# A graph-network kernel on one NeuronCore: new hand-written step orders for three engines

## The chip, the cores and the metric

The kernel runs on one core of a Trainium2 chip. A core has five engines that run their own instruction streams side by side: TensorE (PE in the profile), VectorE (DVE), ScalarE (ACT), GpSimd (POOL) and SyncE (SP, which here only issues loads). They tell each other by semaphores that a buffer is ready or free. The metric is device time in microseconds (us) of one execution; less is better. All 64 graphs are computed by this one core.

## The reference, cut to what matters

The input is 64 graphs of 128 nodes with 64 features each, a 0/1 adjacency matrix per graph, and a node mask. Four graph layers follow one another, each with a residual and a normalisation over the features:

```
x = layernorm(x + PNA(x, adj))            # mean, max, min, std over the neighbours; then a linear layer
x = layernorm(x + adj @ (x @ W) + bias)
x = layernorm(x + MLP(x + quantiles(x, dilated adj)) * mask)   # 0.25/0.5/0.75 quantiles over few neighbours
x = layernorm(x + (adj + I) @ x / rowsum)
```

Max and min over the neighbours (layer 1) and the quantiles over the neighbours (layer 3) are the costly parts: both gather each node's neighbours by rank with one-hot matmuls. Layer 3 then sorts up to 11 gathered values with a sorting network.

## The kernel before

The 64 graphs are worked on in eight groups of eight; the code calls a group a turn, t0 to t7. Every layer of a turn is cut into steps, small functions that each issue some instructions on one engine. Three strings at the top of the file, `TENSOR_ORDER`, `SCALAR_ORDER` and `VECTOR_ORDER`, write out the order of the steps on the three engines; `GPSIMD_ORDER` and `SYNC_ORDER` do so for the other two. An entry `name:which@lag` means: in round number n, do step `name` of turn n+lag. So `so:0-20@-1` is the first twenty operations of the sort of the turn before the round's number. Each round repeats the string, entries that name no turn from 0 to 7 are left out, and rounds begin and end so that every step of each turn is done once. This is a software pipeline: while layer 1 of one turn is begun, layers 1 and 2 of the turn before and layers 3 and 4 of the turn before that are finished.

Nothing but these strings sets the order on an engine. Each step begins with waits on semaphores for what it reads and for buffers to be free; an engine that waits does nothing else, and what stands behind the waiting step waits with it.

The steps that matter here, with the lines that the profile shows for them:

- VectorE. `cm` (L1289) masks the adjacency of the next turn; `gt` (L1295), `P` (L1306 to L1309) build the permutation that sorts nodes by degree; `nb`, `mp` (L1323), `rw` (L1332) prepare masks and row factors. `h0` (13 operations, L1362) and `h2` (11 operations, L1370) write one-hot matrices. `dr` (L1344, L1348) finds the dropped neighbours of the dilation. `ng`, `me`, `we` (L1390 to L1394) close mean and variance. `tr:0`, `tr:1` (L1404, L1418) take max and min over gathered slots. `zf:0`, `zf:1` (L1435, L1436) form layer 1's output. `so` (66 operations, L1479) is the sorting network, `wg:0` to `wg:5` (L1492) weigh ranks, `ag` (L1502, L1506) adds them. `z1`, `z2` (L1536), `z3` add the residuals; `n0d` to `n3d` (L1440) and `n0x` to `n3x` (L1444, L1445) are the two VectorE halves of the four normalisations. `r1`, `r2` split x2 for bf16. `em` (L1355) marks empty slots. `pre:k` are set-up steps that only turn 0 has: among them `pre:2` (tables), `pre:3` (weights of the ranks, L1263 to L1282), `pre:4` (degrees of the other 48 graphs, L1143, L1144).
- ScalarE. It empties PSUM and takes squares and roots: `e0:0` to `e0:7` (L912) and `e2:0` to `e2:3` (L921) move gathered slots of layers 1 and 3 to SBUF, two halves each; `ys:0`, `ys:1` (L863) scale layer 1's output; `n0q` to `n3q` (L926) square, `n0r` to `n3r` (L930) take the root; `vt` (L796) and `k2` (L801), `sd` (L896, L898), `y2e` (the rows zB<-rest of L839), `z3e`, `xr`, `ac` (L887), `xh`, `xm`, `xl` (parts of x2), `dtc` (L791), `kn` (whose L780 writes dcol), `pm`, `pl`, `up`, `rp`, `qo`.
- TensorE. `g0:0` to `g0:7` and `g2:0` to `g2:3` gather (two halves each, into two PSUM banks that are used in turn, called the ring; a half may start once the half before last has been emptied); `wr:k` put rank weights into the same ring; `yl:0`, `yl:1` layer 1's linear layer (L445 pna<-bdx,xT is its first matmul); `dt`, `va`, `p2` the dilation; `ss`, `mt` mean and variance; `b1`, `b2` layer 2; `c2`, `c3` (L442 rest<-weights,hT) layer 3's MLP; `c6` layer 4; `kc`, `lv` degrees.
- GpSimd, whose order string is not changed. In each round it does `sk@0` (L1085 to L1093, nine small operations: it needs `kn`'s dcol, and VectorE's `dr` needs it) and then `sc@-2` (L1099, eight indirect DMAs that scatter the finished rows xo to DRAM; it needs `n3x` of that turn). So `sk` of turn n stands behind `sc` of turn n-3.

The last turn's `n3x` is followed by its eight scatters and the end of the program.

Of the kernel before, what the change touches and what calls it, by code (L numbers as in the profile page):

```python
# [134 lines left out]
class Turn:  # L135
# [13 lines left out]


TENSOR_ORDER = """
    g0:1@-1 cr@-1 g0:2@-1 g0:3@-1 kc@0 g0:4@-1 lv@0 g0:5@-1 g0:6@-1 g0:7@-1 yl:0@-1 wr:0@-2 wr:1@-2 yr@0 yl:1@-1
    ap@0 b3@-2 pre:0@0 wr:2@-2 wr:3@-2 xt@0 sm@0 qp@0 wr:4@-2 wr:5@-2 b1@-1 p1@0 b2@-1 q1@0 c2:0@-2 c2:1@-2 q2@0
    dt@0 ss@0 c3@-2 g2:0@-1 va@0 g2:1@-1 p2@0 g2:2@-1 g2:3@-1 c6@-2 g0:0@0 mt@0"""
SCALAR_ORDER = """
    adj@0 n0q@-1 xs@0 n0r@-1 kn@0 b3e@-2 qo@0 up@0 b1e@-1 rp@0 n1q@-1 c2e:0@-2 pm@0 n1r@-1 k1@0 xh@-1 pl@0
    c2e:1@-2 xm@-1 dtc@0 xl@-1 ac@0 e2:0@-1 y2e@-2 vt@0 e2:1@-1 sd@0 n2q@-2 e2:2@-1 n2r@-2 k2@0 e2:3@-1 xr@-2
    e0:0@0 z3e@-2 e0:1@0 n3q@-2 pre:0@2 e0:2@0 n3r@-2 sg@0 e0:3@0 e0:4@0 e0:5@0 e0:6@0 mts@0 e0:7@0 pre:1@0
    ys:0@0 pb@1 ysb@1 ys:1@0"""
VECTOR_ORDER = """  # L160
    so:28-32@-2 gt@0 tr:0@-1 so:32-40@-2 P@0 tr:1@-1 so:40-44@-2 zf:0@-1 so:44-66@-2 wg:0@-2 wg:1@-2 pre:0@0
    zf:1@-1 wg:2@-2 nb@0 n0d@-1 wg:3@-2 pre:1@0 mp@0 n0x@-1 rw@0 wg:4@-2 wg:5@-2 ag@-2 z1@-1 dr@0 n1d@-1
    h2:0-1@-1 pre:2@0 n1x@-1 pre:3@0 h2:1-3@-1 r1@-1 h0:0-1@0 h2:3-4@-1 r2@-1 h0:1-2@0 h2:4-6@-1 h0:2-3@0
    h2:6-8@-1 h0:3-4@0 h2:8-11@-1 h0:4-9@0 me@0 ng@0 we@0 z2@-2 n2d@-2 h0:9-13@0 n2x@-2 pre:5@-1 em@0 pre:4@0
    cm@1 so:0-20@-1 z3@-2 so:20-24@-1 n3d@-2 so:24-28@-1 n3x@-2
    pre:6@-2"""
GPSIMD_ORDER = """
    pre:2@0 pre:0@2 sk@0 pre:1@1 sc@-2 pre:3@-1"""
SYNC_ORDER = """
# [1583 lines left out]
```

## Time and profile before

| | |
|---|---|
| median of 3 runs | 649.8 us (649.49 to 651.43) |
| profiled execution, its own time | 646.34 us |
| its span, first to last instruction | 644.8 us |
| mean granted TensorE clock | 0.874 of full |
| busy: PE, PE weight loads | 482.3 us (75%), 320.0 us (50%) |
| busy: DVE | 514.6 us (80%) |
| busy: ACT | 370.4 us (57%) |
| busy: POOL | 112.8 us (17%) |

Busy time is the time in which an engine had an instruction in work. VectorE is the busiest over the span. From the page's 40 slices one sees a start of some 60 us in which set-up runs, six alike stretches, and a tail of some 70 us in which all engines are half idle. The chain that ended last goes 34% over DVE and 22% over PE. In the timelines, the idle time in front of an instruction and what released it stand in brackets; on DVE and ACT an instruction begins some 0.1 us before the one ahead of it ends.

### The profile page before, as it was taken

The numbers are of one execution on the slowest core, as the hardware profiler recorded it, in microseconds if no ns is written. First come the engines' busy times: TensorE is split into PE (matmuls) and PEld (weight loads), VectorE is DVE, ScalarE is ACT, GpSimd is POOL, SyncE is SP. The second block draws the span as 40 slices with busy tenths as digits, with TensorE's granted clock in tenths as the row PEclk, the third lists the DMA queues.
The fourth block names the chain that finished last, engine by engine and source line by source line (L and its number), as shares of the span: only waits on it lengthen the run. The fifth ranks groups of instructions, "written<-read, shape, count | busy, mean of one in ns | idle before, by whom it ended". The sixth has DMA issues, their size and how long they took to land.

```text
span 644.8 us, 10421 instructions
## 1 busy us (share of the span) xinstructions
PE 482.3 (75%) x3380; PEld 320.0 (50%) x3419; DVE 514.6 (80%) x1504; ACT 370.4 (57%) x990; POOL 112.8 (17%) x186
## 2 busy tenths in 40 slices
PE   2467968797988889798979897989888977861420
PEld 2443655365545655475557554755575545440220
DVE  4895639999799978999899989997999799379220
ACT  0264677447874678568855885588558842440230
POOL 4300010301014100510061006100610070006022
PEclk9866998999899989989998999899989997555555
DMA  8400020002000200020002000200000000000000
GB/s 312 162 0 1 2 82 1 2 1 82 2 4 16 81 2 2 17 83 2 2 16 83 2 1 18 83 2 1 17 2 2 2 17 2 1 0 17 0 6 15
DMA packets 6718, 18.32 MB, mean 28 GB/s; under 512 B 1792, under 2 KB 1920, under 8 KB 6144
## 3 DMA queue, kind: packets, MB, share of 16 engines
q1 hardware_dynamic: 4608, 15.48, 6.8%
q0 software_dynamic: 2048, 2.10, 1.1%
q8 instruction: 28, 0.46, 0.3%
q14 instruction: 34, 0.28, 0.1%
HBM read 15.48 MB, written 2.10 MB: 27 GB/s over the span
## 4 chain that ended last, share of the span: by engine, by line
DVE 34%; issue 27%; PE 22%; ACT 8%; POOL 6%; POOLq 0%; DVEq 0%; ACTq 0%
DVE hot L1479 7%; DVE slot L1479 7%; PE pna L445 6%; DVE slot L1404 5%; PE pna L442 5%; POOL out_dram L1099 5%; PE ring L442 4%; PE relab L442 2%; PE rest L442 2%; DVE deg L1143 1%; ACT wv L863 1%; PE ring L655 1%; DVE slot L1502 1%; DVE P L1309 1%; DVE hot L1492 1%
## 5 line engine op out<-in xcount | busy, mean ns | idle before, releaser
L442 PE MATMUL ring<-hot,parts 128*64 128x384 bf16 (+3 forms) x753 | 137.1, 358 | 0.9
L1099 POOL DMA_INDIRECT out_dram<-xo,idx x64 | 78.1, 1220 | 309.9 <-DVE xo L1445 292.9
L912 ACT ACTIVATE slot<-ring 128x512 f32<-128x512 f32 (+1 forms) x128 | 61.6, 525 | 42.6 <-PE ring L442 38.4
L442 PEld LDWEIGHTS ring<-hot,parts 128*128 128x128 bf16 (+1 forms) x768 | 55.5, 107 | 39.6 <-issue 4.1
L863 ACT ACTIVATE wv<-pna,rowP 128x64 f32<-128x64 f32 x128 | 28.0, 329 | 77.6 <-PE pna L442 77.6
L1404 DVE TENSOR_TENSOR slot<-slot 128x128 f32<-128x128 f32 (+2 forms) x144 | 53.1, 424 | 2.8 <-ACT slot L912 0.9
L1479 DVE TENSOR_TENSOR hot<-slot 128x64 f32<-128x64 f32 (+5 forms) x136 | 50.8, 407 | 3.5 <-ACT slot L921 3.5
L445 PE MATMUL ring<-emp,rowsel 112*128 112x512 bf16 (+1 forms) x128 | 45.3, 354 | 10.9 <-ACT slot L912 7.0
L1479 DVE TENSOR_TENSOR slot<-slot 128x64 f32<-128x64 f32 (+5 forms) x136 | 51.2, 406 | 0.0
L445 PE MATMUL pna<-bdx,xT 128*128 128x384 f32 x64 | 28.6, 530 | 16.5 <-DVE zF L1436 16.5
L921 ACT ACTIVATE slot<-ring 128x384 f32<-128x384 f32 x64 | 31.3, 502 | 15.3 <-PE ring L442 15.2
L442 PE MATMUL pna<-weights,QQ 128*128 128x192 f32 x128 | 36.6, 371 | 0.0
L445 PE MATMUL rest<-x2T,weights 128*128 128x512 f32 x32 | 22.3, 785 | 18.1 <-DVE x2T L1506 10.4
L442 PE MATMUL pna<-wmm,slot 128*128 128x192 f32 x128 | 34.5, 354 | 0.0
L1479 DVE TENSOR_TENSOR hot<-hot 128x128 f32<-128x128 f32 (+3 forms) x96 | 33.6, 378 | 0.0
L1085 POOL TENSOR_SCALAR skp<-dcol 128x2 f32<-128x2 f32 x8 | 2.1, 264 | 175.7 <-ACT dcol L780 175.7
L839 ACT ACTIVATE zB<-rest,rowP 128x64 f32<-128x64 f32 x128 | 28.0, 340 | 6.9 <-PE rest L442 4.0
L445 PE MATMUL ring<-sgnT,delta 32*128 32x512 bf16 (+2 forms) x48 | 14.6, 364 | 22.4 <-DVE slot L1492 20.3
L1479 DVE TENSOR_TENSOR slot<-hot 128x64 f32<-128x64 f32 (+5 forms) x88 | 31.3, 378 | 0.0
L1440 DVE TENSOR_REDUCE stB<-sqB 128x8 f32<-128x512 f32 x16 | 10.9, 683 | 25.2 <-ACT sqB L926 25.2
L445 PEld LDWEIGHTS ring<-emp,rowsel 112*128 112x128 bf16 x128 | 12.9, 101 | 33.8 <-ACT slot L912 22.2
L839 ACT ACTIVATE m<-pna,rowP 128x64 f32<-128x64 f32 x128 | 28.7, 394 | 0.1
(280 smaller groups left out, 1139.1 us busy)
## 6 DMA issues: line engine op xcount, KB each, us to landing
Cc<-adj_cols_dram SPq DMA_DIRECT2D x8, 512.0 KB, 3.8
R<-adj_rows_dram SPq DMA_DIRECT2D x8, 512.0 KB, 5.4
slot<-adj_rows_dram SPq DMA_DIRECT2D x4, 1024.0 KB, 12.4
xn<-x_nat_dram SPq DMA_DIRECT2D x8, 256.0 KB, 5.5
out_dram<-xo,idx POOLq DMA_INDIRECT x64
weights<-wpack_dram SPq DMA_DIRECT2D x1, 608.5 KB, 8.0
biasr<-wrows_dram SPq DMA_DIRECT2D x1, 128.0 KB, 9.4
own_loop<-adj_diag_dram SPq DMA_DIRECT2D x1, 32.0 KB, 15.1
```

Of the source, the lines that this page charges most:

```text
L442: return mm(*a, start=False, stop=True, skip_group_check=True, **k)
L445: return mm(*a, start=True, stop=True, skip_group_check=True, **k)
L655: mm(ps[:, OFF2[k] - lo:OFF2[k] - lo + CAP2[k]], fill2[:, k, :, :].rearrange("p a d -> p (a d)"), sgnT[t.n % KEEP][:, c, 0:CAP2[k]], start ...
L839: last = A(dst[:, g, :], src(g), ACT.Copy, scale=rowP[t.n % ROWKEEP][:, g, which:which + 1])
L863: last = A(ys[:, g, f, :], PQ[:, 256 * g + D * (f + 1):256 * g + D * (f + 2)], ACT.Copy, scale=rowP[t.n % ROWKEEP][:, 4 * h + g, AMP + f:A ...
L912: A(slot0[:, g, lo:hi], PG[ring["g0", t.n, 2 * g + j][0]][:, 0:hi - lo], ACT.Copy).then_inc(s["slot0"], 1)
L921: A(slot2[:, c, lo:hi], PG[ring["g2", t.n, 2 * c + j][0]][:, 0:hi - lo], ACT.Copy).then_inc(s["slot2"], 1)
L1099: nc.gpsimd.indirect_dma_start(out=out, out_offset=bass.IndirectOffsetOnAxis(ap=idx[t.n % ROWKEEP][:, g:g + 1], axis=0), in_=xo[:, g, :], ...
L1143: own(V.tensor_reduce(deg[:, k * CHUNK:(k + 1) * CHUNK], chunk[k], AX.X, ALU.add))
L1404: return V.tensor_tensor(dst, dst, src, ALU.max)
L1440: V.tensor_reduce(st[:, 0, :], sq[:, :, :], AX.X, ALU.add).then_inc(s[signal], 1)
L1479: mark(("sort", k), V.tensor_tensor(low if is_min else wire(b, 1 - sb_, width), low, high, ALU.min if is_min else ALU.max))
```

## The change

Three order strings are replaced. No step is added or left out and no step's body is changed; POOL's and SP's strings stay. The whole diff:

```diff
--- before.py
+++ after.py
@@ -149,21 +149,21 @@
 
 
 TENSOR_ORDER = """
-    g0:1@-1 cr@-1 g0:2@-1 g0:3@-1 kc@0 g0:4@-1 lv@0 g0:5@-1 g0:6@-1 g0:7@-1 yl:0@-1 wr:0@-2 wr:1@-2 yr@0 yl:1@-1
-    ap@0 b3@-2 pre:0@0 wr:2@-2 wr:3@-2 xt@0 sm@0 qp@0 wr:4@-2 wr:5@-2 b1@-1 p1@0 b2@-1 q1@0 c2:0@-2 c2:1@-2 q2@0
-    dt@0 ss@0 c3@-2 g2:0@-1 va@0 g2:1@-1 p2@0 g2:2@-1 g2:3@-1 c6@-2 g0:0@0 mt@0"""
+    p2@-1 g0:0@-1 c6@-3 mt@-1 g0:1@-1 cr@-1 g0:2@-1 g0:3@-1 kc@0 g0:4@-1 g0:5@-1 g0:6@-1 lv@0 g0:7@-1
+    yl:0@-1 yr@0 wr:0@-2 pre:0@0 b3@-2 yl:1@-1 wr:1@-2 ap@0 wr:2@-2 xt@0 wr:3@-2 wr:4@-2 sm@0 wr:5@-2 qp@0
+    b1@-1 q1@0 b2@-1 c2:0@-2 q2@0 p1@0 c2:1@-2 ss@0 dt@0 c3@-2 va@0 g2:0@-1 g2:1@-1 g2:2@-1 g2:3@-1"""
 SCALAR_ORDER = """
-    adj@0 n0q@-1 xs@0 n0r@-1 kn@0 b3e@-2 qo@0 up@0 b1e@-1 rp@0 n1q@-1 c2e:0@-2 pm@0 n1r@-1 k1@0 xh@-1 pl@0
-    c2e:1@-2 xm@-1 dtc@0 xl@-1 ac@0 e2:0@-1 y2e@-2 vt@0 e2:1@-1 sd@0 n2q@-2 e2:2@-1 n2r@-2 k2@0 e2:3@-1 xr@-2
-    e0:0@0 z3e@-2 e0:1@0 n3q@-2 pre:0@2 e0:2@0 n3r@-2 sg@0 e0:3@0 e0:4@0 e0:5@0 e0:6@0 mts@0 e0:7@0 pre:1@0
-    ys:0@0 pb@1 ysb@1 ys:1@0"""
+    e0:2@-1 n3q@-3 e0:3@-1 e0:4@-1 e0:5@-1 e0:6@-1 mts@-1 e0:7@-1 pre:1@-1 ys:0@-1 ysb@0 pb@0 b3e@-2 n3r@-3
+    ys:1@-1 adj@0 n0q@-1 xs@0 kn@0 n0r@-1 qo@0 rp@0 b1e@-1 pm@0 up@0 n1q@-1 c2e:0@-2 pl@0 n1r@-1 k1@0 xh@-1
+    c2e:1@-2 dtc@0 xm@-1 ac@0 pre:0@3 xl@-1 y2e@-2 e2:0@-1 n2q@-2 e2:1@-1 n2r@-2 e2:2@-1 vt@0 e2:3@-1 sd@0
+    k2@0 xr@-2 e0:0@0 z3e@-2 e0:1@0 sg@0"""
 VECTOR_ORDER = """
-    so:28-32@-2 gt@0 tr:0@-1 so:32-40@-2 P@0 tr:1@-1 so:40-44@-2 zf:0@-1 so:44-66@-2 wg:0@-2 wg:1@-2 pre:0@0
-    zf:1@-1 wg:2@-2 nb@0 n0d@-1 wg:3@-2 pre:1@0 mp@0 n0x@-1 rw@0 wg:4@-2 wg:5@-2 ag@-2 z1@-1 dr@0 n1d@-1
-    h2:0-1@-1 pre:2@0 n1x@-1 pre:3@0 h2:1-3@-1 r1@-1 h0:0-1@0 h2:3-4@-1 r2@-1 h0:1-2@0 h2:4-6@-1 h0:2-3@0
-    h2:6-8@-1 h0:3-4@0 h2:8-11@-1 h0:4-9@0 me@0 ng@0 we@0 z2@-2 n2d@-2 h0:9-13@0 n2x@-2 pre:5@-1 em@0 pre:4@0
-    cm@1 so:0-20@-1 z3@-2 so:20-24@-1 n3d@-2 so:24-28@-1 n3x@-2
-    pre:6@-2"""
+    so:24-28@-2 z3@-3 so:28-32@-2 pre:3@-1 so:32-35@-2 gt@0 so:35-38@-2 n3d@-3 so:38-40@-2 tr:0@-1
+    so:43-44@-2 so:40-43@-2 P@0 so:44-47@-2 tr:1@-1 zf:0@-1 so:47-66@-2 n3x@-3 wg:0@-2 pre:0@0 zf:1@-1 nb@0
+    wg:1@-2 wg:2@-2 wg:3@-2 wg:4@-2 n0d@-1 pre:1@0 rw@0 wg:5@-2 n0x@-1 ag@-2 mp@0 pre:2@0 z1@-1 h2:0-2@-1
+    n1d@-1 h2:2-3@-1 n1x@-1 dr@0 r1@-1 h2:3-4@-1 ng@0 h2:4-6@-1 h0:0-3@0 r2@-1 h0:3-6@0 h2:6-8@-1 h0:6-7@0
+    h2:8-11@-1 em@0 h0:7-9@0 z2@-2 h0:9-12@0 me@0 n2d@-2 pre:5@-1 h0:12-13@0 we@0 pre:4@0 n2x@-2 cm@1
+    so:0-24@-1 pre:6@-2"""
 GPSIMD_ORDER = """
     pre:2@0 pre:0@2 sk@0 pre:1@1 sc@-2 pre:3@-1"""
 SYNC_ORDER = """
```

The new strings are also cut at another place: the steps from `so:24-28` on, which stood at the end of a round, now stand at the head of the next round with their lag lowered by one. That alone changes nothing in the sequence that an engine sees. What differs in the sequence, with the lags brought to the same round:

- VectorE: `n3x` goes from behind sort operation 28 to behind the whole sort; `tr:0` and `P` stand later against the sort and `zf:0` directly behind `tr:1`; `wg` 1 to 5 stand behind `zf:1` and `nb`; `n0x`, `mp` and `dr` stand later, with `dr` behind `n1x`; `ng`, `em` and most of `h0` stand earlier; between `z2` and `n2d` now stand three `h0` operations and `me`, and `we` stands behind `n2d`. `pre:3` stands in the second round instead of the first.
- ScalarE: `y2e` goes ahead of `e2:0`; `n2q` goes from behind `e2:1` and `sd` to directly behind `e2:0`; `vt` from ahead of `e2:1` to behind `e2:2`, `sd` behind `e2:3`; `xl` behind `ac`; `pm` ahead of `up`; `b3e` and `n3r` between `pb` and `ys:1`.
- TensorE: `va` goes ahead of `g2:0`, `p2` behind `g2:3`; `ss` goes ahead of `dt`; `p1` behind `q2`; `lv` behind `g0:6`; the `wr` steps are spread between `yr` and `qp`, and `b3` goes ahead of `yl:1`.

## Rows read from the trace of the kernel before

**Rows 1.** Engines' busy time in one steady turn: PE, PEld, DVE, ACT, POOL, clock, DMA, GB/s
```profile
441.00:506.00 65.00, 56.01 (x425) 37.64 (x429) 59.14 (x172) 45.18 (x125) 11.92 (x17) 0.97 0.02 6
```

**Rows 2.** Timeline of DVE in that turn: start, duration, line, operation, idle time before
```profile
473.96 0.69 DVE L1492 TENSOR_TENSOR slot<-slot,ring 128x512 f32<-128x512 f32 x1
...
475.74 0.42 DVE L1435 TENSOR_TENSOR zF<-pna,wv 128x256 f32<-128x256 f32 x1 [0.50 <-ACT wv L863]
...
486.97 0.61 DVE L1348 SCALAR_TENSOR_TENSOR drop<-keyN,skp,drop 128x128 bf16<-128x128 bf16 x2
...
488.86 0.69 DVE L1445 TENSOR_TENSOR x<-zF,stF 128x512 f32<-128x512 f32 x1
...
499.29 0.68 DVE L1536 TENSOR_TENSOR zB<-zB,x 128x512 f32<-128x512 f32 x1
503.58 0.69 DVE L1440 TENSOR_REDUCE stB<-sqB 128x8 f32<-128x512 f32 x1 [3.61 <-ACT sqB L926]
...
506.52 0.23 DVE L1479 TENSOR_TENSOR hot<-slot 128x64 f32<-128x64 f32 x1 [0.36 <-ACT slot L921]
```

**Rows 3.** Timeline of ACT around the longest wait of DVE
```profile
497.09 1.75 ACT L839 ACTIVATE zB<-rest,rowP 128x64 f32<-128x64 f32 x8
499.35 1.02 ACT L796 ACTIVATE validT<-relab 128x1024 bf16<-128x1024 f32 x1 [0.52 <-PE relab L442]
...
502.31 0.72 ACT L898 ACTIVATE m<-wv,eps 128x512 f32<-128x512 f32 x1
502.93 0.61 ACT L926 ACTIVATE sqB<-zB 128x512 f32<-128x512 f32 x1
...
505.50 0.98 ACT L921 ACTIVATE slot<-ring 128x384 f32<-128x384 f32 x2
```

**Rows 4.** Timeline of PE: c3, g2:3 and its last half; then a g2 half of the tail
```profile
492.85 1.90 PE L442 MATMUL rest<-weights,hT 128*128 128x64 f32 x16
...
503.98 0.34 PE L655 MATMUL ring<-sgnT,fill 32*128 32x128 bf16 x3 [0.37 <-ACT slot L921]
...
505.19 0.73 PE L442 MATMUL ring<-hot,parts 128*64 128x424 bf16 x6
...
568.12 1.27 PE L442 MATMUL ring<-hot,parts 128*64 128x424 bf16 x6
```

**Rows 5.** Timeline of POOL: first and last scatter of eight, sk, two scatters of later turns
```profile
452.20 1.07 POOL L1099 DMA_INDIRECT out_dram<-xo,idx  x1 [35.05 <-DVE xo L1445]
...
462.63 1.44 POOL L1099 DMA_INDIRECT out_dram<-xo,idx  x1 [0.30 <-issue]
479.20 0.23 POOL L1085 TENSOR_SCALAR skp<-dcol 128x2 f32<-128x2 f32 x1 [15.13 <-ACT dcol L780]
...
481.83 0.20 POOL L1093 TENSOR_TENSOR skp<-skp 128x2 f32<-128x2 f32 x1
...
524.30 3.69 POOL L1099 DMA_INDIRECT out_dram<-xo,idx  x1 [0.30 <-issue]
...
632.97 0.96 POOL L1099 DMA_INDIRECT out_dram<-xo,idx  x1 [0.30 <-issue]
```

**Rows 6.** Busy time and granted clock during yl:1 of turn 2 and of turn 6
```profile
207.30:211.70 4.40, 4.38 (x24) 3.69 (x25) 4.40 (x18) 0.00 (x0) 0.00 (x0) 1.00 0.01 4
467.90:474.00 6.10, 6.10 (x25) 5.21 (x26) 6.07 (x22) 0.04 (x1) 0.00 (x0) 0.72 0.01 4
```

**Rows 7.** Timelines of DVE and ACT in the start
```profile
38.98 0.29 DVE L1263 TENSOR_SCALAR zB<-steps_of 32x2 f32<-32x2 f32 x3
...
41.62 1.11 DVE L1282 TENSOR_SCALAR delta<-zB,parity 32x576 bf16<-32x576 f32 x2
...
57.19 0.93 ACT L912 ACTIVATE slot<-ring 128x512 f32<-128x512 f32 x2 [4.15 <-DVE rtmp L1144]
...
65.04 0.28 DVE L1295 TENSOR_TENSOR gt<-relab,thr 128x112 bf16<-128x112 f32 x1 [7.29 <-PE relab L445]
...
114.33 0.91 DVE L1479 TENSOR_TENSOR hot<-slot 128x64 f32<-128x64 f32 x1 [1.13 <-ACT slot L921]
```

## The prediction, made before the changed kernel was run

> **What bounds the kernel now.** I read the slices of the page first, then the busy time by windows, then the timelines of the engines over one turn. From turn 2 to turn 6 the program repeats itself: the scatter that starts at 452.20 in [rows 5] has its twin one turn earlier at 387.32, and the first sort operations of turns 5 and 6 lie at 441.65 and 506.52, so one turn takes 64.9 us. In 65.0 us DVE is busy for 59.1, PE for 56.0, ACT for 45.2 [rows 1]. So DVE sets the pace, and what it loses is 5.8 us of waits per turn. The timeline shows where [rows 2]: 3.61 us stand in one place, ahead of n2d (503.58), behind ACT's square n2q; 0.50 ahead of zf:1; 0.36 ahead of the sort; two more of 0.41 (wg:4) and 0.22 (r2); the rest is small change between dependent operations, about 0.5, which any order keeps. The square itself is not slow: ACT had y2e done at 498.84 and z2 followed at 499.29 to 499.97, but n2q began only at 502.93, because in ACT's order vt, e2:1 and sd stand between [rows 3], and e2:1 waits for a gather that PE runs behind va. The wait is one of order, not of work. A new order can therefore give back at most about 5.3 us in each steady turn; with no wait left a turn would take 59.2 + 0.5 = 59.7 us.
>
> **The steady turn in the new order.** I lay DVE's steps back to back and ask at each wait whether the other engines have delivered.
>
> *n2q.* y2e is now ahead of e2:0, n2q directly behind it. From the end of y2e, n2q is done after e2:0 (0.98 in [rows 3]) and its own 0.61, some 1.5 us. DVE has z2 (0.68), three small h0 operations (0.3) and me (0.6) to do in that time, 1.6. So the 3.61 go to nothing. n2x waits for n2r, which is behind e2:1, but we (four operations of 0.7) now covers it.
>
> *y2e and z2.* What is late next is y2e. From the end of dr ACT must do dtc 0.38, xm 0.63, ac 2.7, xl 0.6, y2e 1.75 with hand-overs, 6.4 us; DVE has r1, r2, ng, em, h2:3-11 and h0:0-9 there, which I add up to 5.7. So z2 waits 0.7.
>
> *The sort's start.* It needs e2:3. From c3's start to the end of g2:3 the old order takes 492.85 to 505.92, 13.07 us [rows 4], with p2 in it, which now stands behind; without p2 and its pause of 0.5 it is 12.6. c3 now stands behind dt, dt behind dr: 0.4 more ahead of it, and 0.5 for the last half of e2:3 behind: 13.5 from the end of dr to the sort. DVE's own work there is what it now does from the end of dr (487.58) to z2 (499.29), less n1d, n1x and the h2 operations that now come before dr, 9.2 us, and from z2 to the sort 7.23 less 3.97 of waits, 3.3; with z2's 0.7 that is 13.2. So the sort waits 0.3 to 0.4, as now. PE and DVE are level here; ACT's sd, k2 and mt fall behind and stand beside the sort.
>
> *The scatter: the new wait.* sk and sc are not moved on GpSimd, but n3x is moved on DVE, from behind sort operation 28 to behind the last one, about 23 us later. In the old order the eight scatters end 15 us before sk's input arrives (15.13 idle in [rows 5]). In the new one they start behind the sort and sk stands behind them, and dr needs sk. From xo's end (451.92) the scatters take to 464.07, 12.15 us; sk takes 479.20 to 482.03, 2.83; with hand-overs dr can begin 15.3 us after n3x. DVE's work between: in the old trace wg:0 to the end of n1x is 473.96 to 489.55 [rows 2], 15.6 us; less dr 1.0, less waits of 1.0, plus two h2 operations 0.67, 14.2. So dr waits 1.1. The cost has bounds: eight scatters beside an idle DVE take 10.1 us (0.96 each, the last row of [rows 5], and 0.30 between them), which would hide it whole, 0; single ones take up to 3.69 us, 2.3 more than the usual; if that came in every turn the wait would be 3.4. I take 1.1, from the four alike steady scatters. This wait also hides smaller ones ahead of it: zf:1 (late by 0.7 when PE runs yl:1 slow) and n1x (behind n1r, 0.5).
>
> A rule speaks against this place. The Trainium skill, "SBUF — State Buffer", Who interferes with whom, says that a VectorE tensor_scalar may hold the port pair it shares with GpSimd and so stop the writing of descriptors of a GpSimd DMA. mp (0.69) and the first h2 operations are of that kind and now fall into the scatters' 12 us, where the old order has only tensor_tensor and the like; by the rule a turn would cost up to 1 us more, and the time would be some 5 us above the forecast. No row here shows such a pair.
>
> *yl:1 and the clock.* In turn 6 PE idles 2.3 us ahead of yl:1, then runs it at half clock for part (0.72 mean, 6.03 us); in turn 2 the same idle time is followed by full clock and 4.35 us [rows 6]. Now wr:0 and b3 stand in that gap, and tr:1 is followed by zf:0 at once; I get 1.8 us of idle time. Whether the clock falls or not, at most 1.7 us of yl:1 are at stake, of which DVE sees 0.7 and the scatter's wait takes them. Value 0.
>
> *lv, P, gt.* kc and lv come to 3.2 and 8.0 us after so:24's start, gt and P stand at 4.3 and 11.8 on DVE; wg:k find their wr:k done by some tenths, where wg:4 waits 0.41 today. I count 0.
>
> Sum: 59.7 + 1.1 (dr) + 0.7 (z2) + 0.4 (sort) = 61.9 us a turn, 3.0 less than 64.9. Six such stretches lie between the sort of turn 0 (114.33) and that of turn 6 (506.52): 18.0 us less.
>
> **Start.** ACT's e0:0 of turn 0 waits till 57.19 for pre:4's degrees [rows 7]; ahead of pre:4 ng, em and four h0 operations (1.1) go into time in which DVE waits for ac, and ac itself comes 0.5 earlier because ss is ahead of dt: 1.6 less. pre:3 (38.98 to 42.73, 3.8 us) moves into the 7.29 us in which DVE waits for kc [rows 7], cost 0; it gave nothing on its own, since ac was waited for. In the second round the sort waits for e2:3 till 114.33 [rows 7]; ss no longer stands behind dt and dr, and va and p2 no longer split the g2 steps: 1.1 less. Together 2.7.
>
> **Tail.** After turn 6's sort PE sits at half clock (a g2 half of 1.27 instead of 0.73 us, [rows 4]) and the chain x1, b1, b2, x2, g2, sort sets the end. n3x (0.8) and wg:4, wg:5 (1.1) now stand ahead of the last n0x, less old waits and 0.4 saved ahead of zf:0: 0.8 more. What follows, sort to last scatter, is the same chain.
>
> Total: 18.0 + 2.7 - 0.8 = 19.9 us less. The profiled execution took 646.3 us, so 626.4 for its like; the median of the runs is 3.5 higher, and from it the forecast is 649.8 - 19.9 = 629.9 us.
>
> **Rivals.**
> A, forecast, chance 0.50: 623 to 636, as above with half a microsecond a turn either way and 2 for start and tail.
> B, the new waits vanish too, 0.12: the scatters run in 10 to 11 us and y2e is in time, a turn takes 60.2; 6 x 1.7 less, 620. For it: nothing else is far behind. Against it: the four steady scatters are alike to 0.01 us, and DVE works beside them in either order.
> C, PE becomes the bound between dr and the sort, 0.20: the stretch has 13.5 against 13.2 us, without slack, and the gaps around b1, b2, c2 lie just ahead of it. If the clock falls there, g2 steps take 3.3 instead of 1.9 us; over one such spell that is 1.5 us a turn, 6 x 1.5 more, 639; with a second wait of that size, 643. Against it: the same gaps stand in the old order at full clock. The Trainium skill, "TensorE: Matmul & The Clock Gate", Part 1, calls the window in which activity is looked at free-running, so that the same gap need not have the same effect; yl:1 of turns 2 and 6 agrees with it.
> D, slower, 0.13: the scatters hold up dr. It is one mechanism: scatters, sk, dr in a row behind n3x. Each microsecond by which they are longer than 12.15 is a microsecond of every turn. Even with the old time at a turn of 64.9 when they take 15.2; if two of eight are as slow as the one of 3.69, they take 16.7, a turn 66.4, and the time is 649.8 + 6 x 1.5 - 1.9 = 657. For it: the sets of turns 5 and 6 each have one of over 3.5 us. Against: no steady turn has.
> E, no change, 0.05: the wait ahead of n2d only moves, to z2 and the sort in full.
>
> The range holds A, most of C and nearly B: 619 to 644. By 0.3% (2 us, about what the runs tell from no change) faster takes A, B, C: 0.80 after a small part of C that ends level; same 0.06; slower 0.14.
>
> **What will show it.** In the changed trace: the distance of two equal steps some turns apart, 61.9; n2d without a wait; an idle time of about 1 us ahead of dr, with sk's L1093 as its releaser and sk's first operation directly behind the eighth scatter; z2 0.7 behind ACT's zB; the sort 0.4 behind e2:3; DVE busy for 95% of a turn. Wrong would be: dr waiting 3 us or more (D), half clock in c3, va or g2 of the middle turns (C), or a turn of 60 (B).

## The result, and the profile after

The changed kernel takes 619.9 us in the median of four executions (616.0, 624.7, 615.3, 623.8), the kernel before 649.6: a ratio of 0.952 (95% interval 0.942 to 0.961). Six more executions of it gave 622.4 and a ratio of 0.956 (0.952 to 0.960). I had forecast 629.9 us, with a range of 619 to 644. The sign and the main mechanism were right; the gain in the medians, 29.7 us, was half as large again as the 19.9 us of my sum. The profiled execution took 616.0 us, its span 614.3 us, 30.5 less than the 644.8 before.

Where the 30.5 us lie, by the first sort operation of each turn (VectorE, L1479) in the two traces:

| stretch | before | after | difference | forecast |
|---|---|---|---|---|
| start to the sort of t0 | 114.33 | 115.22 | +0.9 | -2.7 |
| t0 to t2 | 132.65 | 120.68 | -12.0 | -6.0 |
| t2 to t6, four turns | 259.54 | 245.91 | -13.6 | -12.0 |
| sort of t6 to the end of the span | 138.24 | 132.51 | -5.7 | +0.8 |

One steady turn first: two neighbouring turns of after (busy time of PE, PEld, DVE, ACT, POOL, then clock, DMA share, GB/s; the twin of [rows 1]).

```profile
358.88:419.76 60.88, 54.42 (x428) 36.41 (x427) 58.81 (x171) 45.20 (x124) 10.81 (x17) 1.00 0.08 27
296.78:358.88 62.10, 55.75 (x429) 37.62 (x428) 58.92 (x172) 45.18 (x124) 10.40 (x17) 0.97 0.08 27
```

VectorE does what it did, 58.8 us, in 60.9 us instead of 64.9. In the turn of 62.1 the clock was half for a short time behind 332.4, in qp; b2 came later and z1 waited 1.10 us for it. VectorE's timeline in the faster turn (start, duration, line, operation, idle before), to be held against [rows 2]:

```profile
404.60 0.20 DVE L1444 RECIPROCAL stF<-stF 128x8 f32<-128x8 f32 x1 [0.23 <-ACT stF L930]
404.83 0.70 DVE L1445 TENSOR_TENSOR x<-zF,stF 128x512 f32<-128x512 f32 x1
405.46 0.41 DVE L1344 TENSOR_SCALAR drop<-keyN,skp 128x128 bf16<-128x128 bf16 x2
...
412.98 0.69 DVE L1536 TENSOR_TENSOR zB<-zB,x 128x512 f32<-128x512 f32 x1 [0.78 <-ACT zB L839]
...
414.65 0.69 DVE L1440 TENSOR_REDUCE stB<-sqB 128x8 f32<-128x512 f32 x1
...
419.76 0.23 DVE L1479 TENSOR_TENSOR hot<-slot 128x64 f32<-128x64 f32 x1
```

The wait of 3.61 us ahead of n2d has gone, z2 waits 0.78, and dr at 405.46 does not wait at all. ScalarE in the same place: y2e at 411.22, then e2:0, then the square n2q at 414.00, 1.05 us behind y2e's end instead of 4.1 [rows 3].

```profile
411.22 1.73 ACT L839 ACTIVATE zB<-rest,rowP 128x64 f32<-128x64 f32 x8
412.79 0.54 ACT L921 ACTIVATE slot<-ring 128x384 f32<-128x384 f32 x1
...
414.00 0.62 ACT L926 ACTIVATE sqB<-zB 128x512 f32<-128x512 f32 x1
```

GpSimd, the first and the last two of the eight scatters, then the first and the last operation of sk (twin of [rows 5]):

```profile
391.38 1.07 POOL L1099 DMA_INDIRECT out_dram<-xo,idx  x1 [48.89 <-DVE xo L1445]
...
399.06 1.24 POOL L1099 DMA_INDIRECT out_dram<-xo,idx  x1 [0.30 <-issue]
400.61 0.96 POOL L1099 DMA_INDIRECT out_dram<-xo,idx  x1 [0.30 <-issue]
401.59 0.50 POOL L1085 TENSOR_SCALAR skp<-dcol 128x2 f32<-128x2 f32 x1
...
404.80 0.19 POOL L1093 TENSOR_TENSOR skp<-skp 128x2 f32<-128x2 f32 x1
```

sk does stand directly behind the eighth scatter, as forecast. But from the end of xo (391.09) to the end of the scatters pass 10.5 us and not 12.15, so sk is done at 404.99, half a microsecond ahead of dr.

The start, ScalarE's e0:0 of turn 0 and the end of VectorE's path to the first sort (twin of [rows 7]), with GpSimd beside it:

```profile
54.85 0.93 ACT L912 ACTIVATE slot<-ring 128x512 f32<-128x512 f32 x2 [3.39 <-DVE rtmp L1144]
```

```profile
107.97 1.54 DVE L1391 TENSOR_TENSOR wv<-wv,m 128x512 f32<-128x512 f32 x1
...
115.22 0.23 DVE L1479 TENSOR_TENSOR hot<-slot 128x64 f32<-128x64 f32 x1 [1.63 <-ACT slot L921]
...
124.22 0.82 DVE L1479 TENSOR_TENSOR hot<-slot 128x64 f32<-128x64 f32 x2
```

```profile
107.46 1.50 POOL L1069 TENSOR_TENSOR xo<-rows,rowsb 128x384 f32<-128x384 f32 x1
...
111.85 1.19 POOL L1072 CAST rowsb<-xo 128x384 bf16<-128x384 f32 x1
```

The first sort operation takes 0.23 us, where it took 0.91 in [rows 7]. What has moved is a one-off job of GpSimd, the split of the row factors (L1068 to L1072, released by pre:5): before it ran from 112.3 to 118.3 beside the sort, now it runs from 106.5 beside `we`, whose operations take 1.2 to 1.5 us instead of 0.69.

```profile
112.31 1.60 POOL L1068 CAST rowsb<-rows 128x384 bf16<-128x384 f32 x1 [19.75 <-DVE rows L1159]
```

This is the split's first operation in the trace of the kernel before.

The end: granted clock in the stretch with g2 of turn 7, first in this execution, then in a later one of the same kernel that took 623.6 us.

```profile
530.00:540.00 10.00, 9.73 (x111) 5.97 (x111) 3.94 (x12) 7.16 (x20) 0.00 (x0) 1.00 0.01 2
```

```profile
530.00:540.00 10.00, 9.50 (x61) 6.38 (x63) 3.46 (x11) 5.26 (x15) 0.00 (x0) 0.50 0.01 2
```

### The profile page after: what moved, and what is told of

It is laid out like the page before. It is cut to its first block, busy times and chain, and to the rows that moved or that the text cites. A ratio compares the mean times of both kernels' runs of the same rounds, so it can differ in the third digit from the quotient of the medians.

```text
span 614.3 us, 10460 instructions
## 1 busy us (share of the span) xinstructions
PE 470.8 (77%) x3419; PEld 310.6 (51%) x3419; DVE 513.0 (84%) x1504; ACT 370.9 (60%) x990; POOL 103.5 (17%) x186
## 4 chain that ended last, share of the span: by engine, by line
issue 63%; POOL 14%; DVE 9%; PE 7%; ACT 4%; POOLq 0%; DVEq 0%; ACTq 0%
POOL out_dram L1099 10%; PE ring L442 3%; DVE hot L1479 2%; PE pna L445 2%; DVE slot L1479 2%; DVE deg L1143 1%; PE pna L442 1%; ACT m L839 1%; DVE slot L1404 1%; ACT QQ L887 1%; PE ring L445 1%; PE ring L655 1%; ACT wv L863 1%; POOL skp L1085 0%; POOL skp L1088 0%
## 5 line engine op out<-in xcount | busy, mean ns | idle before, releaser
L442 PE MATMUL ring<-hot,parts 128*128 128x328 bf16 (+3 forms) x768 | 139.8, 358 | 0.0
L1099 POOL DMA_INDIRECT out_dram<-xo,idx x64 | 63.9, 998 | 369.7 <-DVE xo L1445 352.7
L912 ACT ACTIVATE slot<-ring 128x512 f32<-128x512 f32 (+1 forms) x128 | 62.5, 525 | 30.4 <-PE ring L442 27.0
L1479 DVE TENSOR_TENSOR hot<-slot 128x64 f32<-128x64 f32 (+5 forms) x136 | 49.2, 391 | 5.4 <-ACT slot L921 4.9
L1479 DVE TENSOR_TENSOR slot<-slot 128x64 f32<-128x64 f32 (+5 forms) x136 | 49.9, 396 | 0.0
L921 ACT ACTIVATE slot<-ring 128x384 f32<-128x384 f32 x64 | 32.7, 512 | 19.3 <-PE ring L442 18.9
L445 PE MATMUL ring<-sgnT,delta 32*128 32x512 bf16 (+2 forms) x48 | 17.2, 359 | 26.6 <-DVE slot L1492 23.3
L442 PE MATMUL pna<-weights,QQ 128*128 128x192 f32 x128 | 33.8, 346 | 0.0
L1479 DVE TENSOR_TENSOR hot<-hot 128x128 f32<-128x128 f32 (+3 forms) x96 | 33.2, 373 | 0.0
L442 PE MATMUL pna<-wmm,slot 128*128 128x192 f32 x128 | 31.6, 329 | 0.0
L1479 DVE TENSOR_TENSOR slot<-hot 128x64 f32<-128x64 f32 (+5 forms) x88 | 31.1, 375 | 0.0
L445 PE MATMUL rest<-x2T,weights 128*128 128x512 f32 x32 | 19.9, 707 | 11.5 <-ACT hT L984 6.8
L655 PEld LDWEIGHTS ring<-sgnT,fill 32*128 32x128 bf16 x352 | 16.3, 95 | 22.0 <-ACT slot L921 13.4
L655 PE MATMUL ring<-sgnT,fill 32*128 32x128 bf16 (+5 forms) x352 | 25.1, 198 | 1.2 <-ACT parts L979 0.9
```

What stands on the lines that cost most here:

```text
L442: return mm(*a, start=False, stop=True, skip_group_check=True, **k)
L445: return mm(*a, start=True, stop=True, skip_group_check=True, **k)
L655: mm(ps[:, OFF2[k] - lo:OFF2[k] - lo + CAP2[k]], fill2[:, k, :, :].rearrange("p a d -> p (a d)"), sgnT[t.n % KEEP][:, c, 0:CAP2[k]], start ...
L912: A(slot0[:, g, lo:hi], PG[ring["g0", t.n, 2 * g + j][0]][:, 0:hi - lo], ACT.Copy).then_inc(s["slot0"], 1)
L921: A(slot2[:, c, lo:hi], PG[ring["g2", t.n, 2 * c + j][0]][:, 0:hi - lo], ACT.Copy).then_inc(s["slot2"], 1)
L1099: nc.gpsimd.indirect_dma_start(out=out, out_offset=bass.IndirectOffsetOnAxis(ap=idx[t.n % ROWKEEP][:, g:g + 1], axis=0), in_=xo[:, g, :], ...
```

## The experiments

Each was run beside the kernel before on the same chip; its median there lay between 648.6 and 649.8 us.

**The changed kernel again.** No edit.

> The changed kernel once more, word for word. Its four runs so far lie at 615.3 and 616.0 us with a mean clock near 0.897, and at 623.8 and 624.7 us with a clock near 0.868, with nothing between. Theory 1: the program has no second path; what differs is where TensorE's granted clock falls to half. Then the runs here fall into the same two groups (615 to 617 and 623 to 625), and this trace, whichever group it is of, shows the same steps in the same order with DVE's waits the same to 0.2 us wherever the clock is the same, and the difference to the first trace sits in stretches with the clock at 0.5. Rival: the runs differ in the scatters or the loads; then steady turns would differ in length with the clock at 1.00.

622.4 us (615.6 to 623.6), ratio 0.956 (0.952 to 0.960). Up to the sort of turn 6 the profiled execution is the one of the first trace to within 0.3 us: turns of 60.90, 62.08, 60.89, 62.09. Then the clock is half from 517.2 to the end, g2 steps of turn 7 take 3.29 instead of 1.94 us, and the sort of turn 7 begins 65.8 us after that of turn 6 instead of 58.4. That one stretch is the whole difference between the 616.0 and the 623.6 us, as the last two rows above show. In this execution the stretch from the sort of t6 to the end takes 139.8 us, 1.6 more than before, where the first trace has 5.7 less. My theory had the runs fall into the two groups 615 to 617 and 623 to 625. That did not come true: four of the six took 621.3 to 622.7 us, between the two, at mean clocks of 0.875 to 0.883; none of these four has a trace.

**Only the wait of n2q, in the kernel before.**

```
-    ... e2:0@-1 y2e@-2 vt@0 e2:1@-1 sd@0 n2q@-2 e2:2@-1 ...
+    ... y2e@-2 e2:0@-1 n2q@-2 vt@0 e2:1@-1 sd@0 e2:2@-1 ...      (ScalarE, kernel before)
```

> The kernel before, with ScalarE's y2e put ahead of e2:0 and n2q directly behind e2:0; nothing else moves. Theory 1 (orders fit together): n2q comes at 500.0 instead of 502.9 of the turn, DVE's wait of 3.61 ahead of n2d falls to about 0.7, but ScalarE then does vt, e2:1, sd, e2:2, k2 and e2:3 that much later, and the sort waits for e2:3 at about the old time (506.5): a turn stays at 64.5 to 64.9 and the time at 646 to 650 us. Rival (the wait is n2q's place alone): 2.9 us less in each of six turns, 632 us.

650.5 us, ratio 1.0024 (1.0002 to 1.0047). VectorE's waits in one turn:

```profile
505.85 0.69 DVE L1440 TENSOR_REDUCE stB<-sqB 128x8 f32<-128x512 f32 x1 [0.76 <-ACT sqB L926]
...
510.15 0.20 DVE L1444 RECIPROCAL stB<-stB 128x8 f32<-128x8 f32 x1 [3.21 <-ACT stB L930]
```

The wait of 3.61 has become one of 0.76 for the square and one of 3.21 for the root n2r, further on in the same normalisation: n2r still stood behind vt, e2:1 and sd. To take away one wait of order gives nothing while the next step of the same chain stands behind the same things.

**Only that undone, in the changed kernel.**

```
-    ... y2e@-2 e2:0@-1 n2q@-2 e2:1@-1 n2r@-2 e2:2@-1 vt@0 e2:3@-1 sd@0 ...
+    ... e2:0@-1 y2e@-2 vt@0 e2:1@-1 n2q@-2 e2:2@-1 n2r@-2 e2:3@-1 sd@0 ...      (ScalarE)
```

> The changed kernel with ScalarE's order around the gathers put back in part: e2:0 ahead of y2e, vt ahead of e2:1, n2q behind e2:1. Theory 1: e2:0 then waits for g2:0, y2e ends 2.6 us later, n2q is done 3.4 us later, and DVE waits that much ahead of z2 and n2d with we, n2x, cm and the sort behind it: a turn of 60.9 becomes 64.0 to 64.5, the time 637 to 643 us. Rival (the new order of TensorE, with va ahead of g2:0, is what shortened the turn): a turn stays under 62 and the time under 628.

643.2 us, ratio 0.991 (0.987 to 0.995): 21 to 23 us above the changed kernel, three quarters of the gain. The edit puts back the places of y2e and vt together with that of n2q. Steady turns take 64.1 to 65.3 us; in the one that starts at 376.02 VectorE waits

```profile
432.94 0.69 DVE L1536 TENSOR_TENSOR zB<-zB,x 128x512 f32<-128x512 f32 x1 [3.58 <-ACT zB L839]
435.16 0.69 DVE L1440 TENSOR_REDUCE stB<-sqB 128x8 f32<-128x512 f32 x1 [0.62 <-ACT sqB L926]
```

So most of the loss now stands ahead of z2, 3.58 us: y2e, which z2 needs, is again behind e2:0, and e2:0 waits for the first gather. It is the place of y2e and n2q together that is worth these microseconds, and not that of n2q alone.

**Only TensorE's new order, in the kernel before.** The edit is the first block of the diff, alone.

> The kernel before with TensorE's new order alone; ScalarE and VectorE as before. Theory 1 (a turn of 64.9 is set by VectorE and by the wait of 3.6 us for n2q, which is one of ScalarE's order): the turn moves by less than 1 us, as the gathers ahead of e2:1 come 0.5 us sooner without p2 among them; 645 to 652. Theory 2 (TensorE's order is what gives the gain): a turn near 62 and 630 or less.

694.1 us, ratio 1.068 (1.064 to 1.073): neither theory, a turn of 71.7 us, 6.8 more than before. ScalarE, then VectorE, at the start of one sort (481.58):

```profile
479.64 1.11 ACT L801 ACTIVATE key<-relab,not_member 128x1024 bf16<-128x1024 f32 x1 [3.67 <-PE relab L445]
480.65 0.90 ACT L921 ACTIVATE slot<-ring 128x384 f32<-128x384 f32 x2
```

```profile
481.58 0.23 DVE L1479 TENSOR_TENSOR hot<-slot 128x64 f32<-128x64 f32 x1 [3.60 <-ACT slot L921]
```

ScalarE's old order has k2 ahead of e2:3. k2 needs p2, and TensorE's new order puts p2 behind the last gather: ScalarE waits 3.67 us for it, e2:3 stands behind, the sort waits 3.60. In the changed kernel k2 stands behind e2:3. This wait is 3.2 of the 6.8 us; the rest is in smaller ones, 1.66 ahead of z2, 0.92 ahead of z3, 0.76 ahead of r1, while n2d still waits 2.81. I had costed "p2 behind g2:3" at half a microsecond of gain; it is that only together with ScalarE's order.

**n3x ahead, so that no scatter stands ahead of sk.**

```
-    ... so:47-66@-2 n3x@-3 wg:0@-2 ...
+    ... so:28-32@-2 n3d@-3 ... so:35-38@-2 n3x@-3 ... so:47-66@-2 wg:0@-2 ...      (VectorE; n3r moved ahead on ScalarE)
```

> The changed kernel with n3d, n3r and n3x put back to the first half of the sort (n3x behind sort operation 37, before max and min), so that the scatters run beside sort and max/min as in the kernel before, and sk has no scatter ahead of it. Theory 1: what runs on DVE beside the scatters sets their length: eight of them take 12.1 us here against 10.46 in the changed kernel, where they lie beside wg, zf, reduces and ag. Since dr does not wait for sk in the changed kernel, the turn stays at 60.9 and the time within 2 us of the changed kernel's in the same state of the clock. Rival 1 (the scatters are shorter for another reason than DVE's operations): 10.5 here too. Rival 2 (the scatters or sk hold up the changed kernel after all): 1 us a turn less, 6 us in all.

628.6 us in the median, from 614.6 to 635.2; its executions differ too much in granted clock for a ratio. The turns can be read: 61.00 three times, against 60.9 and 62.1. So n3x behind the sort costs nothing. The same scatters, now beside the sort and tr:1 (a_n3x_early, GpSimd, the last two of the eight):

```profile
387.51 3.35 POOL L1098 DMA_INDIRECT out_dram<-xo,idx  x1 [0.30 <-issue]
391.17 1.15 POOL L1098 DMA_INDIRECT out_dram<-xo,idx  x1 [0.30 <-issue]
```

take 13.5 us from xo's end in each of four turns, against 10.5 behind the sort and 10.1 at the end of the program, beside an idle VectorE. So the place decides, as theory 1 said, but its 12.1 was too low. The loads are not the reason: in the changed kernel the eight take 10.5 us whether the DMAs move 148 GB/s meanwhile (329.0 to 339.5) or 22 (451.9 to 462.4), and where they take longer, in the kernel before and in this run, it is 17 to 21. Which of VectorE's operations lengthens them these runs do not say, and ScalarE's and TensorE's work moved against the scatters as well. One stretch of it, t1 to t2, took 68.8 us instead of 61.9: the clock was half through the gathers.

```profile
229.90:243.60 13.70, 13.70 (x94) 5.90 (x94) 7.41 (x22) 7.38 (x19) 0.00 (x0) 0.50 0.00 1
```

**sk longer.**

```
-                own(V.tensor_scalar(skp[:, 0, :], m, 0.5, 0.25, ALU.mult, ALU.add))
+                for _ in range(7):
+                    own(V.tensor_scalar(skp[:, 0, :], m, 0.5, 0.25, ALU.mult, ALU.add))
```

> The changed kernel, with the first operation of sk on GpSimd done seven times instead of once, some 2.1 to 2.4 us more between the last scatter and dr. Theory 1 (scatters, sk, dr stand in a row behind n3x, and this row ends about 0.4 us ahead of DVE's own work, because the scatters take 10.46 and not 12.15 us): dr waits 1.7 to 2 us behind sk, of which the wait of n1x or of z2 takes a few tenths away; a steady turn of 62.3 to 62.9, the time 9 to 12 us longer, about 631. That would be near what I forecast for the change, with scatters of 12.15. Theory 2 (the row has more slack, or TensorE's row to the sort sets the turn): the turn stays within 0.5 us of 60.9 and the time within 3 us.

633.0 us, ratio 0.974 (0.969 to 0.980), 11 to 13 above the changed kernel. Turns of 62.7 and then 62.1; GpSimd's first operation of sk, then VectorE:

```profile
410.28 2.33 POOL L1086 TENSOR_SCALAR skp<-dcol 128x2 f32<-128x2 f32 x7
```

```profile
415.50 0.42 DVE L1345 TENSOR_SCALAR drop<-keyN,skp 128x128 bf16<-128x128 bf16 x2 [1.28 <-POOL skp L1094]
```

From the eighth scatter's end to sk's end pass 5.2 us instead of 3.4; with these 1.7 us more in the row, dr waits 1.28 us and the turn grows by 1.2. That is the wait that I had forecast for scatters of 12.15 us, made by hand. That the whole time, too, is near my 629.9 is chance: about 5 us of it are one more stretch of half clock through the gathers of turn 1 (t0 to t1 took 65.6 instead of 58.8).

**GpSimd's split back beside the sort.** pre:5 on VectorE from ahead of h0:12 to behind so:24-28.

> The changed kernel, with the one-off step pre:5 on VectorE moved from ahead of the end of h0 in turn 1 to behind sort operation 28, so that GpSimd's split of the rows, which it releases (6 us), lies beside the sort of turn 0, as it does in the kernel before, and no longer beside we of turn 1. Theory 1 (GpSimd's tensor_tensor and VectorE's with two SBUF inputs slow each other, as sort operations of 0.91 instead of 0.23 us in the kernel before show): we of turn 1 takes 2.9 again instead of 5.8, which the sort's wait hides; some sort operations behind 28 take three to four times their time, and the whole is 4 to 7 us longer than the changed kernel: about 3 for the work of pre:5, which now stands on the path, and 2.5 to 3 for the slowing. Theory 2 (the slow sort operations had another cause): only the 3 us of pre:5, sort operations of equal length.

626.7 us, ratio 0.968 (0.963 to 0.973), 4 to 7 above. VectorE and GpSimd:

```profile
127.97 1.80 DVE L1478 TENSOR_TENSOR hot<-slot 128x64 f32<-128x64 f32 x2
```

```profile
127.71 1.38 POOL L1068 TENSOR_TENSOR xo<-rows,rowsb 128x384 f32<-128x384 f32 x1
```

The same two sort operations took 0.82 in the changed kernel (124.22 above). Seven sort operations took 5.7 instead of 2.4 us, pre:5 itself 2.9; the stretch t0 to t1 grew by 6.8. With this the 0.91 of [rows 7] is explained: VectorE and GpSimd slow each other. The Trainium skill, "SBUF — State Buffer", Who interferes with whom, says that a VectorE instruction with two SBUF inputs contends with a GpSimd instruction that reads SBUF; these rows agree.

**The split ahead of z1.** pre:5 moved to ahead of z1 of turn 0.

> The changed kernel, with the one-off step pre:5 moved to ahead of z1 of turn 0, where VectorE waits 3.4 us for b2 (the kernel with matmuls added shows that wait at 89.1 to 92.5). GpSimd's split of the rows then runs at 92 to 98, beside z1, x1 and dr and no longer beside we. Theory 1 (the sort of turn 0 starts when TensorE's g2 steps end, at half clock about 114.9, so VectorE's work ahead of it is covered): VectorE comes to the sort some 5 us earlier (2.9 of pre:5, 2.9 of the slow we) and waits these 5 us; sort of turn 0 at 114 to 115.5, the time as the changed kernel's, 615 to 623. Theory 2 (VectorE and the slowed we decide the start): the sort at 110 to 112 and 3 to 5 us less.

628.3 us, ratio 0.968 (0.964 to 0.973). Neither theory: slower by 6 to 8 us. The sort waited 8 us, as theory 1 said, but began at 116.25. VectorE, then TensorE:

```profile
92.19 2.34 DVE L1369 TENSOR_SCALAR hot<-key 128x1024 bf16<-128x1024 bf16 x2
...
116.25 0.22 DVE L1478 TENSOR_TENSOR hot<-slot 128x64 f32<-128x64 f32 x1 [7.99 <-ACT slot L920]
```

```profile
98.21 0.27 PE L444 MATMUL relab<-identb,drop 128*128 128x128 bf16 x2 [2.68 <-DVE drop L1347]
```

The two h2 operations took 2.34 us beside the split, elsewhere 0.75; dr came later and TensorE, which needs it, idled 2.68 us. The 1 us at the sort is this. The profiled execution (625.1 us, clock half from 518.6 to the end) is then 1.5 us above the 623.6 of the changed kernel with such a tail; two others took 631 us, which no trace explains.

**Matmuls in TensorE's idle gaps of the last turns.** They write a PSUM bank that nothing reads any more.

```
+            def wt(t, k):
+                for _ in range(LATE[k].get(t.n, 0)):
+                    new(PT[:, 512:1024], rows3[:, :], biasb[:, 0, :])
```

> The changed kernel, with matmuls added whose result nobody reads, in TensorE's idle gaps of the last turns only: 6, 6, 6, 2, 3, 3 of them around yl:1, wr:2, b1, b2 of turn 7 and c2, c3 of turn 6, then 84 ahead of wr:2 of turn 7, 16, 3, 3 around c2 and c3 and 20 ahead of c6 of turn 7. They leave the output as it is. Theory 1 (TensorE's clock decides the tail: half clock from about 517 to the end costs the four g2 steps of turn 7 5.4 us and c2, c3, c6 5.5 us): granted clock full through g2 of turn 7 in every execution, g2 steps 1.94 us; c3 3.9 to 2.0, c6 3.7 to 2.0, so 610 to 616 in every run, 5 to 9 below the middle of the runs of the changed kernel (about 621), and no second group of runs near 622. Theory 2 (the two groups come from something else, the DMAs or a slower chip, and the clock only shows it): times as before, 615 to 623 in two groups, or slower where the added matmuls delay the chain.

607.4 us (605.9 to 610.1), ratio 0.938 (0.935 to 0.941): all six executions within 4.2 us, 12 to 15 us below the medians of the changed kernel. TensorE in the tail, and the clock from 540 to 560 with the 84 matmuls:

```profile
533.67 0.68 PE L443 MATMUL ring<-hot,parts 128*64 128x384 bf16 x6
...
538.66 18.08 PE L446 MATMUL relab<-biasb,rows 128*128 128x512 bf16 x82 [0.16 <-issue]
...
569.45 1.89 PE L443 MATMUL rest<-weights,hT 128*128 128x64 f32 x16
```

```profile
540.00:560.00 20.00, 17.77 (x81) 7.78 (x81) 19.94 (x61) 1.42 (x3) 1.92 (x2) 1.00 0.01 2
```

t6 to t7 takes 56.3 us, and from the sort of t7 to xo 48.1 instead of 53.6: c3 runs in 1.9 us, where the changed kernel has 3.5:

```profile
575.91 3.51 PE L442 MATMUL rest<-weights,hT 128*128 128x64 f32 x16
```

The clock is an input of the tail and not a symptom. I had expected 610 to 616; I had left out that ahead of t7's gathers yl:1 and b2 gain as well, 2 us.

**The same in the start and ahead of every yl:1.**

> As the kernel with matmuls added in the last turns, and in addition 5 of them ahead of yl:1 in turns 0 to 6 (idle gap 1.5 us), and 4, 4, 4, 2, 2, 3 ahead of b1 and b2 of turn 0, ss, dt, va of turn 1 and g2:0 of turn 0, where the clock was half from about 97 to 117. Theory 1 (the clock costs 5.4 us in g2 of turn 0, of which the sort sees some 4, and 1.2 us in each of the two turns of 62.1 us instead of 60.9): 3 to 7 us below the kernel with the last turns alone, 604 to 611; every steady turn 60.9. Theory 2 (the start is set by VectorE and ScalarE, and a spell of half clock in a steady turn has another cause, or the added matmuls cost TensorE as much as they give): within 2 us of the kernel with the last turns alone.

608.3 us (604.9 to 615.7), ratio 0.938 (0.934 to 0.942): no better. Of its four steady turns three took 60.9 us and one 62.1, exactly as in the kernel filled only in the tail, so nothing shows that the matmuls ahead of yl:1 did anything. The clock was full in g2 of turn 0, whose last half ended at 109.1, but the sort began only at 113.40:

```profile
110.69 1.54 DVE L1416 TENSOR_TENSOR wv<-wv,sqF 128x512 f32<-128x512 f32 x1
112.15 1.33 DVE L1311 TENSOR_SCALAR key<-Cc 128x1024 bf16<-128x1024 f32 x1
113.40 0.21 DVE L1501 TENSOR_TENSOR hot<-slot 128x64 f32<-128x64 f32 x1
```

Here it is VectorE that comes late, because of `we` beside GpSimd's split. The half clock had hidden that.

**That kernel with pre:5 ahead of z1.**

> The same move of pre:5 on top of the kernel with matmuls added in the gaps of the start, of every turn and of the tail (608.3; its g2 steps of turn 0 end at 109.1 at full clock, but its VectorE reaches the sort only at 113.4, with we at 5.7 us instead of 2.9 beside GpSimd's split). Theory 1 (two covers lie on each other: half clock hides the slow we, the slow we hides the half clock): the sort of turn 0 at 109.8 to 110.3, some 3.3 us less than without the move, 603 to 606 in the fastest runs, the middle about 605. Theory 2 (a third row, ScalarE's k2 or e2, ends at 113 as well): within 1 us of 608.

612.2 us, ratio 0.943 (0.939 to 0.947): not the 605 of theory 1, and in the median 4 us more. dr's delay left TensorE idle for 2.27 us, the clock was half from 98.5 to 119 in spite of the added matmuls, and the sort of t0 began at 117.60.

**That kernel with pre:5 and the split both under idle time.**

```
-    ... pre:0@0 zf:1@-1 ...    n2d@-2 pre:5@-1 h0:12-13@0 ...      (VectorE)
+    ... pre:0@0 pre:5@-1 zf:1@-1 ...    n2d@-2 h0:12-13@0 ...
-    pre:2@0 pre:0@2 sk@0 pre:1@1 sc@-2 pre:3@-1      (GpSimd)
+    pre:2@0 pre:0@2 pre:3@-1 sk@0 pre:1@1 sc@-2
```

> The kernel with matmuls added in the gaps of the start, of every turn and of the tail (608.3), with pre:5 moved on VectorE to ahead of zf:1 of turn 0, where VectorE waits 6.3 us for ScalarE (76.2 to 82.6), and GpSimd's split of the rows (pre:3) moved ahead of sk of turn 1, so that it runs at about 79 to 85, beside an idle VectorE and no longer beside h2 and dr, where it cost 2.3 us. Theory 1 (the start is held by two covers, half clock in g2 of turn 0 and the we slowed by the split; both must go): we of turn 1 at 2.9 us, dr where it was (95.8), g2 of turn 0 at full clock, the sort of turn 0 at 109.8 to 110.3 instead of 113.4, and 603 to 606, the lowest of all. Theory 2 (the clock falls in the start whatever is put into the gaps, or sk of turn 1 and dr come later behind the split): the sort at 113 or later and no gain.

607.0 us (604.4 to 611.0), ratio 0.935 (0.931 to 0.939), the lowest median, though within the scatter of the 607.4. The start is as theory 1 had it:

```profile
106.40 0.69 DVE L1415 TENSOR_TENSOR wv<-wv,sqF 128x512 f32<-128x512 f32 x1
...
110.33 0.23 DVE L1500 TENSOR_TENSOR hot<-slot 128x64 f32<-128x64 f32 x1 [2.63 <-ACT slot L942]
```

3.1 us earlier. The profiled execution gave it back in t2 and t4, which took 65.45 us. The first row is such a turn, the second the same stretch of the turn between them:

```profile
283.40:296.40 13.00, 12.66 (x96) 5.85 (x97) 7.38 (x21) 7.22 (x21) 0.00 (x0) 0.56 0.01 3
344.30:357.30 13.00, 12.79 (x133) 7.94 (x134) 11.94 (x35) 11.13 (x33) 0.00 (x0) 1.00 0.01 1
```

## Why the prediction was right or wrong

The sum gave 19.9 us; the two traces differ by 30.4 in the table. Of the 10.5 us between them, 6.5 lie in the tail, 6.0 between t0 and t2 and 1.6 in the four steady turns, and the start takes 3.6 back. The terms that failed are the tail's 0.8 us of loss, which rested on half clock, and dr's wait of 1.1 us in every turn; beside them the start's 2.7 us of gain, and a slow sort in the first turn that the sum left out.

*The bound, and n2q: right.* VectorE set the pace, and its wait ahead of n2d went to 0; undoing y2e's and n2q's places costs 21 to 23 us. What my sum did not say is that the new orders only work together: two parts of the change alone gave +1 and +44 us.

*y2e and z2: right.* 0.7 forecast, 0.78 and 0.80 measured.

*The sort's start: right in kind.* 0.3 to 0.4 forecast, 0.10 measured, n1x 0.23 beside it.

*dr behind the scatters: the failed step of the steady turn.* I took 1.1 us, "from the four alike steady scatters" of 12.15 us. The measured wait is 0, because the eight take 10.5 us where they now stand; a turn at full clock takes 60.9 and not 61.9. The order in the queue was right, and with 1.7 us more in it the wait is there (1.28). Wrong was that I treated the 12.15 as a property of the scatters. It went with what ran beside them: 13.5 us with the sort and tr:1, 12.15 in the old order, 10.5 behind the sort, 10.1 beside nothing. That it is VectorE's work is the likely reading; no run moved that work alone. The sentence "DVE works beside them in either order" hid that the work would be of another kind. I had given 0 as the lower bound of this wait. This is half of rival B, to which I gave 0.12; B's other half, y2e in time, did not happen, so a turn takes 60.9 and not 60.2.

*The rule of the Trainium skill against this place ("SBUF — State Buffer", Who interferes with whom): not tested.* mp begins at 401.35, only 0.2 us ahead of the end of the eighth scatter, and the first h2 operations fall wholly into sk. So, but for these 0.2 us, no tensor_scalar of VectorE lay beside a scatter, and the extra 5 us had nothing to come from. sk itself took 3.0 to 3.4 us instead of 2.83.

*The turns' number, and what the first turns have of their own.* I took six times 3.0 from t0 to t6. At full clock a turn gained 4.0, since dr does not wait. The four steady turns gave 13.6 and not 16, since two of them had half clock in qp, 1.2 us each. The first two stretches gave 12.0. Of these 8.0 are the same 4.0 a turn. Another 3.0 are the slow first sort operations (8.9 against 5.9 us for the first twenty), which the trace of before showed in [rows 7], 0.91 us in the very row that I quoted, and which I read past. The last 1.0 is in t1 to t2: there VectorE, in the kernel before, waited 3.99 us ahead of n2d instead of 3.61 and 1.14 us for ac, though not the 0.50 ahead of zf:1; in the new order none of these waits is left.

```profile
235.50 0.69 DVE L1382 TENSOR_TENSOR m<-m,QQ 128x512 f32<-128x512 f32 x1 [1.14 <-ACT QQ L887]
```

*Start: wrong by 3.6.* e0:0 did come 2.3 us earlier (1.6 forecast). But g2 of turn 0 ran at half clock, 3.29 us a step and 1.17 to 1.27 us a half, where the old order had full clock and 0.68 to 0.73; the sort waited for it. Behind that stood a second delay of nearly the same length, which the first one hid (a cover, for short): `we` slowed by the split. The clock alone gave 1 to 2 us (113.40 instead of 114.1 to 115.5), both together 4 to 5 (110.33).

*Tail: wrong by 6.5, the largest miss.* I carried "PE sits at half clock" over from the old trace as a fact. In the changed kernel it holds in some executions and not in others; where it holds, g2 alone costs 5.4 us. With the tail at half clock the profiled execution took 623.6 us, and its tail was 1.6 us longer than before, not far from the 0.8 forecast; with g2 of turn 7 at full clock the time was 616.0. So the term failed on the clock that it took for granted; which of the two times an execution shows is luck as far as these runs go. With the gaps filled it is 607.

*Rival C* (half clock in the gathers of a steady turn) did not happen in the changed kernel, but it is real: single stretches of 65.5 to 68.8 us in three of its variants, some 4.5 to 7 us each. I had priced a spell at 1.5 us, by far too low; and twice six times 1.5 is 18, which would have put the rival's upper time at 648 and not 643.

*Rival D* had the right slope: of 1.7 us more in the row 0.5 went into its slack, and the 1.2 left made the turn 1.2 us longer.

What stays open: why the clock falls in one execution of the same program and not in another, and which operation beside the scatters makes them longer.

## What to carry to other kernels

The duration of an operation on GpSimd or VectorE, a scatter's included, is read together with what the other engine does beside it; when a change moves it to another neighbour, take both durations for the range. Ask of each stage which cover lies under the one that is seen, since two covers of equal length make either fix look worthless. A tail with idle gaps on TensorE is worth filling with matmuls that nobody reads: here that gave 12 to 15 us more, half as much as the whole reordering. In the start and in the steady turns the same filling brought nothing that the medians show (608.3 and 607.0 against 607.4).

## What the runs showed of the hardware that I had not expected

- VectorE and GpSimd slow each other: beside GpSimd's split a sort operation takes 0.91 instead of 0.23 us, an operation of `we` 1.54 instead of 0.69, two h2 operations 2.34 instead of 0.75, and of the split itself the first cast 1.60 instead of 0.85 beside an idle VectorE. The eight scatters take 13.5 us beside the sort and tr:1, 10.1 beside an idle VectorE.
- Some 84 matmuls that do no work (82 in the trace), in one gap of some 19 us, kept the clock full and cost the path nothing: the sort beside them ran as before.
- Of one program some executions keep full clock in the tail and some do not; the two differ by 7.4 us, all of it behind the sort of turn 6.
